# Last layer of a four-layer network in two parts: attention of all batches, then blocks of sorted rows with five of eight experts

## The reference, cut to what matters

```python
# third: attention over the 1024 rows of a batch
Q, K, V = X @ W_q + b_q, X @ W_k + b_k, X @ W_v + b_v
A = softmax(Q @ K.T / 16); f = A @ V
# fourth: a shared network and routed experts, on each row by itself
scores = sigmoid(xf @ gate.T)                 # 8 experts, two groups of four
# the better group is kept, the other group's scores become 0, the top two are selected
lat = xf @ fc1_w.T                            # 256 -> 128
out_e = relu2(lat @ w1[e].T) @ w2[e].T        # 128 -> 128 -> 128, only the two selected experts count
f = (sum of selected out_e, weighted) @ fc2_w.T + relu2(xf @ up_w.T) @ down_w.T   # shared: 256 -> 1024 -> 256
```

## Time and profile before

| | |
|---|---|
| median of three executions | 1962.0 us |
| profiled execution | 1953.67 us |
| its span, first to last instruction | 1951.9 us |
| granted TensorE clock, mean | 0.982 of full |
| stage_c, first TensorE instruction to the end | 714.0 to 1951.9 us |
| time from batch to batch in stage_c | 150.1 us |

### The profile page before, as it was taken

The page is one execution under the profiler, slowest core; times in us unless marked ns, Lnnn a source line. Parts: engine busy times, 40 slices in busy tenths (PEclk is TensorE's granted clock), DMA queues, the critical chain, the costliest instruction groups (busy, mean ns, idle before and its releaser), DMA issues.

```text
span 1951.9 us, 35230 instructions
## 1 busy us (share of the span) xinstructions
PE 1831.9 (94%) x11574; PEld 1618.4 (83%) x11576; DVE 1374.0 (70%) x3272; ACT 872.4 (45%) x1625; POOL 861.0 (44%) x1166
## 2 busy tenths in 40 slices
PE   7999998599999989999999999999989989989996
PEld 6888887389999977788788888878878878878885
DVE  5788888644444556786786886886886786786674
ACT  4455554433333424445445445455455445445443
POOL 4267777631111142454354354364265255255054
PEclk9999999699999989999999999999999999999998
DMA  4211222323222331111111121121112112111011
GB/s 153 69 65 65 84 90 88 106 89 98 98 86 86 110 98 45 66 44 61 48 68 46 50 81 45 44 79 53 44 51 81 41 47 88 37 51 55 12 44 65
DMA packets 81926, 133.29 MB, mean 68 GB/s; under 512 B 11360, under 2 KB 62432, under 8 KB 81664
## 3 DMA queue, kind: packets, MB, share of 16 engines
q1 hardware_dynamic: 72272, 105.23, 16.1%
q0 software_dynamic: 9520, 26.36, 5.5%
HBM read 105.84 MB, written 25.72 MB: 67 GB/s over the span
## 4 chain that ended last, share of the span: by engine, by line
PE 59%; DVE 8%; issue 6%; POOL 3%; ACT 3%; DMA 0%; DVEq 0%; POOLq 0%; ACTq 0%
PE c_ps L118 9%; PE c_ps L119 9%; PE c_ps L120 9%; PE b_ps L118 5%; PE b_ps L120 5%; PE b_ps L119 5%; PE c_ps L133 3%; PE c_ps L134 3%; PE c_ps L135 3%; PE c_ps L2088 2%; PE c_ps L2134 2%; PE c_ps L2136 2%; PE c_ps L2135 2%; POOL c_pool_tmp L97 1%; ACT b_win_raw L1650 1%
## 5 line engine op out<-in xcount | busy, mean ns | idle before, releaser
L1587 POOL TENSOR_TENSOR c_place<-c_shared_place,c_place 128x512 fp32r<-128x512 f32 x256 | 323.8, 1294 | 188.6 <-ACT c_place L1766 119.2
L1578 POOL DMA_INDIRECT c_gathered<-expert_results,c_slots x112 | 112.2, 1002 | 325.2 <-DVE c_pre L1822 301.7
L1992 DVE SCALAR_TENSOR_TENSOR c_shared_place<-c_ps,c_shared_place 128x512 f32<-128x512 f32 x256 | 169.5, 682 | 44.5 <-ACT c_shared_place L1758 44.4
L118 PE MATMUL c_ps<-c_place 128*128 128x264 f32 (+1 forms) x520 | 151.1, 291 | 16.1 <-DVE c_place L1905 11.6
L1766 ACT ACTIVATE c_place<-c_shared_place 128x512 fp32r<-128x512 f32 x128 | 80.3, 630 | 177.1 <-DVE c_shared_place L1992 175.2
L133 PE MATMUL c_ps<-c_downT_hi,c_place 128*128 128x256 f32 x512 | 146.9, 287 | 8.0 <-POOL c_place L1587 8.0
L119 PE MATMUL c_ps<-c_place 128*128 128x264 f32 (+1 forms) x520 | 148.6, 286 | 0.0
L120 PE MATMUL c_ps<-c_place 128*128 128x264 f32 (+1 forms) x520 | 148.4, 285 | 0.0
L134 PE MATMUL c_ps<-c_downT_lo,c_place 128*128 128x256 f32 x512 | 145.4, 284 | 0.0
L135 PE MATMUL c_ps<-c_downT_hi,c_place 128*128 128x256 f32 x512 | 145.1, 283 | 0.0
L1064 POOL DMA_INDIRECT b_xs<-x_rows,expert_tokens x56 | 57.9, 1034 | 196.7 <-PE b_ps L1252 174.2
(11 more groups left out here) (430 smaller groups left out, 6079.1 us busy)
## 6 DMA issues: line engine op xcount, KB each, us to landing
c_x2T<-score_rows SPq DMA_DIRECT2D x64, 512.0 KB, 5.2
b_win_raw<-xT SPq DMA_DIRECT2D x8, 1024.0 KB, 6.6
a_x_rows<-x SPq DMA_DIRECT2D x8, 1024.0 KB, 5.6
x_rows<-a_x SPq DMA_DIRECT2D x8, 1024.0 KB, 4.5
c_pre<-x_rows SPq DMA_DIRECT2D x8, 1024.0 KB, 5.8
out<-b_win_raw SPq DMA_DIRECT2D x16, 512.0 KB, 3.0
b_win_raw<-w_in SPq DMA_DIRECT2D x7, 1024.0 KB, 5.5
b_wout_raw<-w_out SPq DMA_DIRECT2D x7, 1024.0 KB, 6.0
```

Source lines behind the costliest of these rows:

```text
L118: pe.matmul(out, lh, rh, start=(j == 0), stop=False)
L1578: pool.indirect_dma_start(rows[:, a, :], None, d["ys"], bass.IndirectOffsetOnAxis(ap=slots[:, a, t:t + 1], axis=0), bounds_check=TRASH + P ...
L1587: pool.tensor_tensor(hid_lo[:, place, :], square[:, place % RING, :], f32(hid_hi[:, place, :]), ALU.subtract).then_inc(hid_split, 1)
L1992: v.scalar_tensor_tensor(square[:, place % RING, :], ps[:, s_bank(unit, k - lag), :], 0.0, factor, ALU.max, ALU.mult).then_inc(s_free, 1)
```

## The change

`stage_c` is written anew in two parts. Part one runs attention for batches 0 to 7 with nothing of the fourth sublayer between them. While batch b is in attention, the rows of batch b-1 are normalised and routed (`logits`, `route_a` to `route_c`), and each gets a class (`class`): its group of experts. A count over rows gives each row its place (`pos`: two small matmuls; `count_lower` on GpSimd): rows of the lower group from the front, of the upper group from the end of a new array in memory, `sorted`, to which GpSimd scatters them by indirect DMA (`scatter`), 270 numbers each: the row, its scores and its row number. Part two runs 16 blocks (`u`) of 512 rows. Block 0 is the first half of batch 7, straight from on-chip memory, with all eight experts. Blocks 1 to 14 hold rows of one group and use five experts: the group's four and the first of the other group. Block 15 holds the border between the groups and uses eight. A small `table` computed on chip tells SyncE which rows and which expert weights to load for a block (`load_block`, `load_round`). GpSimd scatters results to `out` by row number (`store`).

The loops are gone: all engines' programs are written out. GpSimd and ScalarE take over `combine` (`weigh`: ScalarE multiplies both gathered rows; `add_results`: GpSimd adds them); gathering has four buffers instead of two. `x3T` and `scoreT` of block u+1 stand among the experts of block u, `out` of block u among the `up` of block u+1. `probT` has two buffers.

```diff
+    def both(u):
+        return u in (0, UNITS - 1)
+    def picks(u):
+        return EXPERTS if both(u) else PICKS
+    def experts_of(u):
+        units, quarter = [], 0
+        for k in range(picks(u)):
+            units.append(("w1", u, k))
+            for _ in range(1 if both(u) or k < 2 else 2):
+                units.append(("down", u, quarter))
+                quarter += 1
+            if u == 0 and k == 2:
+                units.append(("pos", LATE_POST))
...
+            if 0 < u < UNITS - 1 and k in (2, 3):
+                units.append((("x3T", "scoreT")[k - 2], u + 1))
...
+            for j in range(TILES - 3):
+                units += [("score", b, j + 2), ("turn", b, j + 1), ("mix", b, j)]
+                if j == 4 and b:
+                    units.append(("pos", b - 1))
+            if b < LAST:
+                units += [("score", b, 7), ("x2T", n, 0), ("turn", b, 6), ("mix", b, 5), ("x2T", n, 1), ("q", n, 0), ("q", n, 1),
+                          ("turn", b, 7), ("mix", b, 6), ("score", n, 0), ("q", n, 2), ("q", n, 3),
+                          ("mix", b, 7), ("v", n, 0), ("score", n, 1), ("v", n, 1), ("v", n, 2), ("v", n, 3), ("turn", n, 0)]
...
+            ups = [("up", u, k) for k in range(UPS)]
+            units += ups[0:2] + ([("out", u - 1)] if u else []) + ups[2:4] + ([] if u else [("scoreT", 0)]) + [("latent", u)] + ups[4:UPS] + experts_of(u)
...
+            def add_results(b, t):
+                n, rows, two = TILES * (b - 1) + t, x_of(b)[:, t, 0:C], gathered[t % GATHER]
+                pool.wait_ge(weighed, n + 1)
+                pool.tensor_tensor(two[:, 0, :], two[:, 0, :], two[:, 1, :], ALU.add).then_inc(combine_chain, 1)
+                pool.wait_ge(combine_chain, n + 1)
+                pool.tensor_tensor(rows, rows, two[:, 0, :], ALU.add).then_inc(combined, 1)
```

1510 lines of the change are left out of this document (880 added, 630 removed).

## The result

| | changed kernel | kernel before, same chip |
|---|---|---|
| median (lowest to highest, number of executions) | 1982.01 us (1981.2 to 1985.42, 4, one of them profiled) | 1961.47 us (1960.61 to 1962.52, 4, none profiled) |
| ratio, 95% interval | 1.0102 [1.009, 1.0114] | |
| profiled execution, its span | 1985.42, 1983.7 us | 1953.67, 1951.9 us |

The change makes the kernel 1.0% slower; 1879 us had been forecast. To read all later numbers: runs that are taken together on one chip, with the kernel before beside them, I call a sitting, and there turned out to be two kinds of them, which the kernel before shows as 1961 to 1965 us or as 1954.6 to 1955.7 us; the changed kernel took 1982 and 1983 us in the first kind and 1953 us in the second. Ratios are always to the kernel before of the same sitting.

A forecast was written before the change was run, and what follows sets the result against it. TensorE's own instructions were taken as the bound. From the span of 1951.9 us: experts -58.7, `pos` +1, stalls -27, end +2, giving 1869; 1.8 outside the span gives 1871, the 8.3 median distance 1879. Range 1845 to 1932.

The forecast's parts named there:

- What TensorE's work costs: Kernel before, last stage: attention 65.8 us a batch, an eight-expert half 37.6; together 141.0 of a batch's 150.1.
- what is removed: Fourth sublayer: three experts go in 14 of 16 blocks, 252 matmuls of 512 columns, 58.7 us off TensorE.
- part two: Five-expert blocks: TensorE stays the bound at 33.4 us; VectorE 22, GpSimd 21, ScalarE under 18.
- 0.7 us of stall a block: Blocks of part two: TensorE stalls, tightest at the layernorm ahead of the first expert; 11 us in all, bounds 0 and 4.5 each.
- I take 3 us of stalls a batch, 24 in all (bounds 1 and 10): Attention in part one: TensorE's stalls from late queues and from `x2T` waiting about 1.4 us for its norm.
- VectorE ends up to 3.4 us behind, of which a score computed one step ahead covers most: Attention, steps two to five: 14.1 us of other VectorE work in 10.8 of slack, the lateness mostly hidden.
- The seam: Block 0, between attention and part two: 5 us waiting at `pos`, 9 us in all with load and splits, bounds 2 and 20.
- Rival A: Attention: GpSimd's additions delay small VectorE operations, 7 us more a batch, 1935 us in all; chance 0.2.
- Part two starves: Part two: SyncE's queue delivers scores or rows late; at 7 us a block the kernel takes 1977 us; chance 0.06.
- denser than I think: Whole kernel: attention loses 1 us a batch, blocks nothing, the seam 3, giving 1844 us; chance 0.1.
- Loops: Last stage's loop ends: VectorE's 1.84 us a turn is off the path, nothing counted; taken in full, 11 us.
- The median of the runs lies 8.3 above the profiled execution, and I let the change keep that distance.: Whole kernel, last step of the sum: 8.3 us carried over, from 1871 us for the execution to 1879.

The follow-up runs named there:

- e13_after_again: The changed kernel itself, unaltered, run again in the second kind of sitting: 1953.1 us, ratio 0.9981.
- e1: Changed kernel with VectorE's attention order altered: row maximum first, routing and statistics behind it and spread, class and `pos` later: 2019.6 us, ratio 1.0272.
- e5: Changed kernel with VectorE's, ScalarE's and TensorE's attention orders altered, the next batch's `x2T` moved behind the last turned tiles: 2003.4 us, ratio 1.0202.
- e14_values: The order of e8_full with the second score between the second and third value products, last batch's positions and routing a tile later: 1903.9 us, ratio 0.9739.
- e4: Changed kernel with GpSimd's two adds of gathered rows on one column in place of 256: 1959.5 us, ratio 0.9969.
- e12: The order of e8_full with GpSimd's two adds on one column in place of 256, second kind of sitting: 1910.5 us, ratio 0.9773.
- e9_straight: The kernel before, with the four hardware loops over batches of its last stage written out: 1964.4 us, ratio 1.0008.
- e7: Changed kernel with one exchange: in a batch's first five tiles VectorE takes maximum, shift and turned halves ahead of routing and statistics: 1982.2 us, ratio 1.0096.
- e10_full_small: The order of e8_full with GpSimd's two adds on one column in place of 256, first kind of sitting: 1937.1 us, ratio 0.9875.
- e8_full: Changed kernel with all engines' attention orders and the seam reordered, GpSimd's gathers and row scaling earlier: 1922.5 us, ratio 0.9835.

## Why the prediction was wrong

The sum forecast a span of 1869 us. Undisturbed, in `e13_after_again`, it is 1952.4, 83.5 more; in the first trace 114.8 more.

- **What TensorE's work costs, what is removed, part two: right.** Blocks stand 34.8 us apart (forecast 34.1), with VectorE at 21.89 (22) and GpSimd at 20.63 (21). The 58.7 us of dropped experts did come off. The term "0.7 us of stall a block" was 1.4 (34.8 less 33.4): 10 us over 14 blocks.
- **The step that failed: "I take 3 us of stalls a batch, 24 in all (bounds 1 and 10)".** Undisturbed, seven batches take 531.6 us, which is 10.1 a batch above TensorE's work of 65.8, and in the first trace 557.1, or 13.8. Seven times 68.8 had been forecast, so 50 us are missed here, more than half of 83.5. The budgets behind it were met (VectorE 55.1 of a forecast 56, GpSimd 46.5 of 48, ScalarE 42 of 49). What failed is the reading of them: "VectorE ends up to 3.4 us behind, of which a score computed one step ahead covers most". It doesn't, because the next exponential, the turned tile and `mix` all hang on the late maximum in turn. I had seen that steps two to five hold 14.1 us of other work in 10.8 of slack; the trace shows them at 8.9, 8.3, 10.2 and 7.5 us in place of 6.6, a sum of 8.5. Each part in a queue was late for a reason of its own (`e1` to `e5`), and each that was relieved handed the wait to the next. That with another order the same instructions take 68.9 us a batch, 3.1 above TensorE's own 65.8, shows that order is the whole of the miss in this term, and that 3 us a batch was a fair size for a good order and none for this one.
- **What a wait costs was counted once.** The clock had no term. A wait of 3.45 us is followed by a stretch at a granted clock of 0.60; over the seven batches of `e13_after_again` the clock is 0.98, some 10 us in 531.6, and 1.00 in `e14_values`. That cost is inside the 10.1 a batch, not beside it.
- **The seam: 9 us forecast, about 19.** Block 0 takes 56.8 us against 47 (37.6 and 9). `pos` waited 3.7 us, as forecast (5), but the scores for block 0 waited 3.6 to 3.8 behind the layernorm of the last tiles, which I hadn't seen, and GpSimd's splits 4.5.
- **Rival A** (attention becomes the bound of its own part) got 0.2. By its text, small VectorE operations held up by GpSimd's adds and a batch 7 us longer, it is nearest to what came: operations of 0.65 to 0.78 us are there, and the adds are worth 4.7 us a batch in the changed kernel (`e4`) and 1.7 in a good order (`e12`, in the other kind of sitting). Its condition, a full VectorE, was not met. The Trainium skill (GPSIMD Engine Reference, Key points) says that the two share their SBUF interfaces and that a VectorE instruction with two SBUF inputs, or in a 2-port mode, contends; the trace agrees, with 0.78 us against 0.22 for the same operation, and in block 0, beside splits of 1.29 us, 1.24 (`c_key<-c_key,c_falling`). An operation with one on-chip tensor as input is held as well: `c_expd<-c_expd` takes 0.18 us in the last batch and 1.17 beside the splits of block 0; which mode it ran in, no row shows.
- **Part two starves, denser than I think:** neither came. SyncE's queue of copies, scores and rows kept up with blocks of 34.8 us.
- **Loops: right** that nothing is gained (`e9_straight`, 1.0008). The 11 us that the rule of the Trainium skill (Runtime: NRT & Kernel Launch, Instruction fetch mechanics) would give in full didn't show.
- **"The median of the runs lies 8.3 above the profiled execution, and I let the change keep that distance."** It was no constant: the profiled execution of the kernel before has no pause in stage two and fits the second kind of sitting, its plain runs the first. For the changed kernel the same circumstance costs 29 us. Of the 103 us between forecast and result, 83.5 are the sum's, 31.3 the disturbance, 8.3 had been allowed for it, and 3.4 is that the profiled execution was the slowest of the four. Of the 83.5, 50 are the batches, 10 the blocks and 10 the seam; 2.5 lie ahead of the first exponential (757.0 us after 754.5), and the other 11 are not taken apart here.

The prediction's own test had been "Wrong if a batch takes over 72 us with VectorE above 90% busy". The batch did, VectorE stood at 69%. Its other sign, small VectorE operations of over 0.5 us, came true: some ten in a batch.

## What to carry to other kernels

Compare each engine's work with the time step by step, not batch by batch: an engine that is 69% busy set the pace here because the work was bunched ahead of the one instruction on which three others hung. When a stage's independent filler work is taken away (here the fourth sublayer), the stalls that it used to hide have to be costed afresh, and each reordering has to be followed to the next queue, since e1, e5 and e7 each removed a wait and gave all of it back. And take experiments that differ by 1% together: `e10_full_small` and `e8_full`, from different sittings, pointed the wrong way.

## What was not expected of the hardware

One program, same instructions, took 1953 or 1982 us depending on the sitting; one chip was used in a sitting of each kind, so it isn't simply the chip. The loss sits in pauses of TensorE, mostly 0.4 to 0.8 us of idle time with no semaphore to wait for, just after GpSimd has issued eight indirect DMAs in a row, and in the lower clock behind them (0.60 for 4.2 us); it isn't there in 600.7 us of blocks, which have four in a row. That TensorE's instruction fetch is what stops is only a guess: no view shows it. The Trainium skill (Runtime: NRT & Kernel Launch, Instruction fetch mechanics) says that each sequencer fetches its instructions through a DMA queue of its own, mostly hidden. By that a slower fetch would hurt where DMA traffic is dense. The places don't bear this out by the amount of traffic: the blocks move 102 GB/s and lose nothing, stage two moves 96 and does. What differs between sittings stays open. A version with fewer waits lost half as much (15 us); why was not tried.
